# TensorE's slot re-ordered in a two-layer attention kernel: transposed probabilities first, out-projections behind them, the next scores ahead of the weighting of values

## What is computed

```python
h = tok(x, W)                                             # (64, 49, 768) @ (768, 192)
h = layernorm(h + attn1(h))                               # layer 1
h = layernorm(h + attn2(h))                               # layer 2
# attn1: softmax(q k^T + q rel^T, causal) v, then w_proj
# attn2: probs = softmax(h @ Wg.T + bg); combine = its best two, scattered
#        delta = einsum((h @ A + ba) * combine, Bm) + combine @ bb, times 2
#        qkv = h @ Wqkv.T + bqkv + delta; softmax(q k^T / 4) v, then Wproj
```

## Time and profile before

| what | value |
|---|---|
| runs | 397.36, 398.04, 395.19 us |
| the profiled execution | 395.62 us, of which span 393.8 us, mean granted TensorE clock 0.999 of full speed |
| TensorE matmul busy | 374.1 us, 95% of the span |
| TensorE weight load busy | 327.7 us, 83% |
| VectorE, ScalarE, GpSimd busy | 303.0, 217.8, 126.0 us |
| chain of waits, by engine | TensorE 82%, VectorE 5%, ScalarE 4%, issue 3%, DMA 2%, GpSimd 2% |
| DMA rate in the first two slices of 9.85 us | 265 and 230 GB/s |

### The profile page before, as it was taken

One profiled execution on the slowest core, in us unless ns is written; L12 is line 12 of the kernel. 1 busy time (PEld: TensorE's weight loads), 2 busy tenths in 40 slices (PEclk: granted clock), 3 DMA queues, 4 the chain that ended last, 5 costly groups with the idle time before them and its releaser, 6 DMA issues.

```text
span 393.8 us, 13738 instructions
## 1 busy us (share of the span) xinstructions
PE 374.1 (95%) x5312; PEld 327.7 (83%) x5312; DVE 303.0 (77%) x814; ACT 217.8 (55%) x692; POOL 126.0 (32%) x262
## 2 busy tenths in 40 slices
PE   5989999999999999999999999999999999898984
PEld 5778878988889888988898889888888988777874
DVE  7366678677777878987878888697788888697872
ACT  1245565655646646565655566655664665564542
POOL 1222431431323514232324333342324342323332
PEclk9999999999999999999999999999999999999999
DMA  8623421222132112320022201111011101111111
GB/s 265 230 59 102 136 54 20 71 54 50 17 75 55 25 28 69 100 59 9 17 67 68 67 8 29 19 29 21 21 18 30 27 21 19 19 32 17 27 30 37
DMA packets 49338, 20.68 MB, mean 53 GB/s; under 512 B 41262, under 2 KB 45713, under 8 KB 49274
## 3 DMA queue, kind: packets, MB, share of 16 engines
q1 hardware_dynamic: 45386, 10.04, 12.3%
q10 hardware_dynamic: 3888, 9.77, 7.7%
HBM read 12.57 MB, written 2.41 MB: 38 GB/s over the span
## 4 chain that ended last, share of the span: by engine, by line
PE 82%; DVE 5%; ACT 4%; issue 3%; DMA 2%; POOL 2%; SPq 1%; POOLq 0%; ACTq 0%; DVEq 0%
PE ps L474 11%; PE ps L547 9%; PE ps L574 9%; PE ps L585 7%; PE ps L559 6%; PE ps L596 5%; PE ps L524 4%; PE ps L528 4%; PE ps L526 4%; PE ps L597 4%; DMA add<-in_add 2%; PE ps L504 2%; PE ps L510 2%; PE ps L541 2%; PE ps L617 2%
## 5 line engine op out<-in xcount | busy, mean ns | idle before, releaser
L927 DVE TENSOR_REDUCE psum<-probs 113x12 f32<-113x588 f32 x64 | 48.7, 760 | 35.0 <-ACT probs L778 35.0
L792 ACT COPY pt<-ps 113x339 f32<-113x339 f32 x128 | 50.2, 445 | 34.7 <-PE ps L574 34.1
L901 DVE TENSOR_REDUCE mx<-ps 113x12 f32<-113x588 f32 x64 | 48.7, 761 | 18.4 <-PE ps L547 17.7
L429 POOL TENSOR_SCALAR shift<-mv,rstd 128x1 f32<-128x1 f32 (+1 forms) x50 | 14.0, 280 | 149.7 <-ACT rstd L827 149.7
L474 PE MATMUL ps<-tokw,xs 128*128 128x192 f32 (+1 forms) x300 | 56.3, 336 | 4.1 <-DMA tokw<-in_tokw 3.9
L418 POOL TENSOR_SCALAR kbd<-k,const 64x294 f32<-64x294 f32 x64 | 35.0, 557 | 65.1 <-ACT q L771 62.8
L474 PEld LDWEIGHTS ps<-tokw,xs 128*128 128x128 f32 (+1 forms) x300 | 48.9, 192 | 7.0 <-DMA xs<-in_x 4.3
L574 PE MATMUL ps<-const,probs 113*113 113x113 f32 x384 | 49.8, 266 | 3.0 <-DVE probs L936 2.5
L936 DVE TENSOR_TENSOR probs<-probs,rsum 113x588 f32<-113x588 f32 x64 | 49.8, 778 | 2.2
L908 DVE TENSOR_TENSOR probs<-ps,mx 113x588 f32<-113x588 f32 x64 | 49.4, 772 | 2.2
L574 PEld LDWEIGHTS ps<-const,probs 113*113 113x113 f32 x384 | 44.4, 178 | 7.4 <-issue 6.7
(11 more groups left out here) (93 smaller groups left out, 789.0 us busy)
## 6 DMA issues: line engine op xcount, KB each, us to landing
xs<-in_x ACTq DMA_DIRECT2D x23, 384.0 KB, 4.8
vbd<-vrow SPq DMA_DIRECT2D x160, 18.4 KB
out<-o SPq DMA_DIRECT2D x24, 96.0 KB, 1.7
tokw<-in_tokw ACTq DMA_DIRECT2D x3, 192.0 KB, 3.5
w<-in_w SPq DMA_DIRECT2D x1, 472.5 KB, 4.3
xs<-in_x SPq DMA_DIRECT2D x3, 128.0 KB, 3.3
xs<-in_x SPq DMA_DIRECT2D x1, 384.0 KB, 5.8
add<-in_add SPq DMA_DIRECT2D x1, 361.5 KB, 9.4
```

Source lines behind the costliest of these rows:

```text
L792: nc.scalar.copy(pt[n % 2][:, 3 * half:3 * half + 3, :].rearrange("p g i -> p (g i)"), ps[0:PP, 2 + half, 0:3 * PP]).then_inc(pt_ready[hal ...
L901: nc.vector.tensor_reduce(mx[:].rearrange("p (b h) -> p b h", b=2), score_view, AX.X, ALU.max).then_inc(mx_ready, 1)
L927: nc.vector.tensor_reduce(psum[:].rearrange("p (b h) -> p b h", b=2), probs_view(n), AX.X, ALU.add).then_inc(sum_ready, 1)
```

## The change

1. **TensorE's slot.** It now begins with `transpose_h` and `transpose_probs(n-1)`; `out1` and `out2` follow. The scores of chain n+1 stand ahead of `weigh_values` of chain n-1 (except in `fresh` slots, and chain 63, whose scores are computed in slot 62 right behind the transposes, into banks 4 and 5).
2. **GpSimd.** `block_diagonal(n+2)` goes ahead of `normalise` where its k was projected in an earlier slot.
3. **Start.** x of block 2 is issued by SP ahead of `add1`; x of blocks 3 and 4 by ScalarE only behind the first `take_h`. The embedding of slot 1 is also split around `transpose_h`.
4. **End.** Largest value, subtraction and exponential of chain 63 are done in slot 62 (VectorE before the sum of chain 62; `mx` has two buffers). The out-projection of block 21 moves from slot 62 to 63. Blocks 22 and 24 (`urgent`) project q and k ahead of v, and copy q ahead of v. `keep_busy` uses bank 7.

```diff
@@ planner
-    spread(QKV2, 19, lambda b: (ROUTED[b] + 1, max(ROUTED[b] + 1, SLOT2[first_use(b)] - 2 + (SLOT2[first_use(b)] > len(CHAINS) - 6))))
+    spread(QKV2, 19, lambda b: (ROUTED[b] + 1, max(ROUTED[b] + 1, SLOT2[first_use(b)] - 2 + (len(CHAINS) - 6 < SLOT2[first_use(b)] < len(CHAINS) - 1))))
-OUT2 = [n + 2 + (n + 2 in [m + 2 for m in DONE1]) for n in DONE2]
+OUT2 = [n + 2 + (n + 2 in [m + 2 for m in DONE1] + [len(CHAINS) - 2]) for n in DONE2]
+def urgent(b):
+    return SLOT2[first_use(b)] - QKV2[b] <= 1 or b == BLOCKS - 1
+def score_bank(n):
+    return 4 if n == LAST else 0
@@ sync
             sp.dma_start(w1b[:], w1b_in).then_inc(w1b_loaded, 16)
+            sp.dma_start(xs[:, 2], x[2]).then_inc(x_loaded[2], 16)
             sp.dma_start(add1[:], add1_in).then_inc(add1_loaded, 16)
@@ gpsimd
+                layer, t = attention(n + 2)
+                known = bool(layer and (QKV1 if layer == 1 else QKV2)[block_of(t)] < n)
+                if known:
+                    block_diagonal(n + 2)
                 for b in out1(n):
                     normalise(L1, b, h[0:tokens(b), b, :])
...
-                block_diagonal(n + 2)
+                if not known:
+                    block_diagonal(n + 2)
@@ tensor
             for n in range(FIRST, SLOTS):
                 before, u = attention(n - 1)
-                for b in out1(n):
...
-                    bank6 = out_project(L1, p1, b, SLOT1, bank6)
...
-                split = bool(n <= 0 and turns(n))
+                split = bool(n <= 1 and turns(n))
...
                     transpose_probs(n - 1, bank3)
                     if n >= LAST:
                         keep_busy(3)
+                    if n == LAST - 1:
+                        scores(L2, attention(LAST)[1], LAST)
+                for b in out1(n):
...
+                    bank6 = out_project(L1, p1, b, SLOT1, bank6)
...
+                        bank6 = out_project(L2, p2, b, SLOT2, bank6)
                 for b in turns1(n):
...
+                    if urgent(b):
+                        bank4 = project_qk2(b, bank4)
                     bank5 = project_v(L2, b, values2(b), bank5)
-                    bank4 = project_qk2(b, bank4)
+                    if not urgent(b):
+                        bank4 = project_qk2(b, bank4)
...
+                layer, t = attention(n + 1)
+                fresh = bool(layer == 2 and block_of(t) in qkv2s(n))
+                if layer and not fresh and n + 1 < LAST:
+                    scores(L1 if layer == 1 else L2, t, n + 1)
                 if before == 1:
                     weigh_values(L1, u, n - 1)
...
-                if layer and not fresh:
-                    scores(L1 if layer == 1 else L2, t, n + 1)
@@ scalar
-            for b in range(2, XS):
-                load_x(b)
...
+                if b == 0:
+                    for late in range(3, XS):
+                        load_x(late)
...
                 if before:
                     take_y(n - 1, u)
+                if n == LAST - 1:
+                    exponent(LAST)
@@ vector
+                if n == LAST - 1:
+                    largest(LAST)
+                    subtract(LAST)
```

More of the change, by code:

```diff
@@ L275, in build @@
         pt = [sb(f"pt{u}", [PP, 6, PP]) for u in range(2)]
-        mx = sb("mx", [PP, H])
+        mx = [sb(f"mx{u}", [PP, H]) for u in range(2)]
         psum = sb("psum", [PP, H])
@@ L534, in scores @@
                 if n > 0:
[L535 removed]
+                    if n == LAST:
+                        pe.wait_ge(L2.qk_ready, BLOCKS)
+                        pe.wait_ge(L2.v_rows, BLOCKS)
+                    else:
+                        pe.wait_ge(sub_ready, n)
                 else:
@@ L634, in keep_busy @@
             def keep_busy(count):
-                pe.wait_ge(L2.qk_ready, BLOCKS)
+                pe.wait_ge(hw_ready, BLOCKS)
                 for _ in range(count):
-                    nc.tensor.matmul(ps[:, 4, 0:128], ident, ident, start=True, stop=True)
-            LAST = len(CHAINS) - 1
+                    nc.tensor.matmul(ps[:, 7, 0:128], ident, ident, start=True, stop=True)
             bank3 = bank4 = bank5 = bank6 = None
@@ L677, in _ @@
                         keep_busy(3)
+                    if n == LAST - 1:
+                        scores(L2, attention(LAST)[1], LAST)
+                for b in out1(n):
+                    if b == 0:
+                        pe.wait_ge(p1_loaded, 16)
+                        pe.wait_ge(ones_ready, 1)
+                    bank6 = out_project(L1, p1, b, SLOT1, bank6)
+                bare = bool(routers(n) and not turns(n) and not qkv2s(n) and not embeds(n))
+                if not bare:
+                    for b in out2(n):
+                        if b == 0:
+                            pe.wait_ge(p2_loaded, 16)
+                        if n > LAST:
+                            keep_busy(2)
+                        bank6 = out_project(L2, p2, b, SLOT2, bank6)
                 for b in turns1(n):
@@ L836, in _ @@
                     take_ht(b)
-                if n <= 0 and turns(n):
+                if n <= 1 and turns(n):
                     for b in embeds(n):
@@ L845, in _ @@
                     act.wait_ge(masks_ready, 1)
-                if layer:
+                if layer and n < LAST:
                     exponent(n)
@@ L850, in _ @@
                 for b in qkv2s(n):
-                    take_v(L2, b, 0, SLOT2)
+                    if not urgent(b):
+                        take_v(L2, b, 0, SLOT2)
                     take_k2(b)
-                    if turns(n) or embeds(n):
+                    if turns(n) or embeds(n) or urgent(b):
                         take_q2(b)
+                    if urgent(b):
+                        take_v(L2, b, 0, SLOT2)
                 for b in turns(n):
                     take_v(L1, b, NB, SLOT1)
-                if not (n <= 0 and turns(n)):
+                if not (n <= 1 and turns(n)):
                     for b in embeds(n):
@@ L861, in _ @@
                     take_y(n - 1, u)
+                if n == LAST - 1:
+                    exponent(LAST)
                 if not turns(n) and not embeds(n):
                     for b in qkv2s(n):
-                        take_q2(b)
+                        if not urgent(b):
+                            take_q2(b)
                 for b in out1(n):
@@ L989, in _ @@
                     router_max(b)
-                if layer:
+                if layer and n < LAST:
                     largest(n)
                     subtract(n)
+                if n == LAST - 1:
+                    largest(LAST)
+                    subtract(LAST)
                 for b in out1(n):
                     add_residual(L1, b)
-                for b in out2(n):
-                    add_residual(L2, b)
+                if n != LAST:
+                    for b in out2(n):
+                        add_residual(L2, b)
                 for b in out1(n):
```

26 lines of the change are left out of this document (8 added, 18 removed).

## The result

| | before | after |
|---|---|---|
| median of 5 runs each | 397.35 us (395.19 to 398.04) | 436.68 us (431.49 to 441.38) |
| profiled execution, its span | 395.6, 393.8 us | 441.38, 439.6 us |
| mean granted clock | 0.999 | 0.958 |

The changed kernel is slower, by a ratio of 1.093 (95% interval 1.087 to 1.099). Two of its five runs, 441.38 (the profiled one) and 439.71 us, fell into a slower state; ratios, and the medians of the table of experiments, leave such runs out (there also single outliers up to 1996 us), and without them the median here is 432.55 us.

The account below looks back on a forecast made before the run. TensorE's issued work plus its few waits was taken as the bound. Terms +14.8 +17.2 -2.4 -2.4 -1.4 = +25.8 us on the profiled 395.6 gave 421.4, named as 421; range 405 to 430 (8 in 10).

Parts of the forecast that it names:

- Odd boundaries, +14.8: Odd slot boundaries: transposes wait barely covered for ScalarE's copy of y out of bank 2; +14.8 us.
- Even boundaries, +17.2: Ends of even slots: transposes wait for bank 3, emptied by take_hw behind take_y and take_q2; +17.2 us.
- The scores ahead, 0 in themselves: Scores ahead of the weighting: same instructions, so no cost in themselves; 0 us, bounds -2 and +2.
- Transposes ahead of out-projections: VectorE's residual comes some 0.7 us later in the slot but stays hidden, as exponential and sum end later.
- second cover, 0.75 us: Out-projection ahead of the transposes, taken to cover ScalarE's take_y for 0.75 us; moving it removes that cover.
- GpSimd and blocks 22 and 24, -2.4: Waits of scores for the block-diagonal k vanish, -3.0 us; late softmax in short slots, +0.6; net -2.4.
- start, -2.4: Kernel start: earlier add1, -1.5 us; half an embedding filling slot 1's wait, -0.9; together -2.4.
- end, -1.4: Last two chains: transposes 2.4 instead of 4.92 us apart, less 1.1 for chain 62; -1.4 us.
- The bound of 2.7 us: Start: most that delaying 0.77 MB of x, at 265 GB/s, could win for add1; up to 2.7 us.
- Only bank 2 costs: Rival: take_hw done in time, so even boundaries lose only 1.6 and some 1 us; 407 us, chance 0.14.
- Faster: Rival: softmax starts 0.5 us earlier, removing TensorE's waits, and the copy yt is hidden; 386 us, chance 0.06.
- It cancels: Rival: waits are a third of the sums, +10 against -6.2 at the ends; 399 us, chance 0.04.

Follow-up runs that it names:

- h: Changed kernel with the bank of the weighted values alternating between 2 and 3, so half of the next transposes goes to a free bank: 420.93 us.
- k: Changed kernel with the alternating bank and ScalarE's take_hw ahead of take_q2 and inverse_deviation: 419.85 us.
- n: Changed kernel with the alternating bank, take_hw ahead of take_q2 on ScalarE, and the transposes of h1 later in the slot: 401.20 us.
- o: Changed kernel with only the transposes of h1 (and take_h1) later in the slot, in another bank in some slots: 419.93 us.
- a: Changed kernel with the scores put back behind the weighting of values, all else of the change kept: 408.04 us.
- b: Kernel before with only the scores moved ahead of the weighting of values: 429.04 us.
- g: Changed kernel with both TensorE orders put back (out-projections first, scores behind the weighting), all else of the change kept: 392.90 us.
- f: Changed kernel with three idle matmuls ahead of the transposes of probabilities in slots 54 to 62: 429.68 us.
- g2: Kernel g with the start's edit undone too: 394.51 us.
- j: Kernel g with the alternating bank for the weighted values: 391.07 us.
- p: Kernel j with the transposes of h1 later in the slot: 386.95 us.
- l: Kernel k with three idle matmuls ahead of the transposes in slots 54 to 62: 422.93 us.

## Why the prediction was right and wrong

- **The step that failed: the end.** The sum has it at about -1.0 us, at the full clock; it took +15.3. What the runs showed in its place stands under "The term that was missing".
- **Odd boundaries, +14.8.** Right in the mechanism and its times (0.98 against 1.07, 2.53 against 2.55). The step also said that `transpose_h1` at 2.55 sets the time wherever there is an out-projection. My expectation for h forgot that, and so did k's; n and o confirm it.
- **Even boundaries, +17.2.** Right: 1.97 against 1.94 at the place measured. The steps forecast for slots 1 to 54 come to 13.6 (odd, without boundaries 55 and 61) + 12.8 (even, without 54 and later) - 0.9 (half an embedding at the first q/k/v) = 25.5. Measured: 24.2.
- **The scores ahead, 0 in themselves.** Too low. Busy time in slots 1 to 54 grew by 2.0 us (301.7 against 299.7), the upper bound that the step gave; from a to the changed kernel, where the scores alone move, it grew by 3.1 (from 298.6). But the prediction took scores and out-projection for two covers of the same copy. By b the scores alone cost nearly all (23.3 us in slots 1 to 54), since the out-projection waits for y too.
- **Transposes ahead of out-projections, "It stays hidden".** The residual was not hidden: TensorE waits 2.9 us for h in a, 1.1 in g. And the "second cover, 0.75 us" was none for `take_y` but one for probabilities and hw: 7.0 us between g and a in slots 1 to 54. The sum of the middle was right all the same, since with both orders changed the waits lie on top of each other. That was luck: nothing in the prediction provided for it.
- **GpSimd and blocks 22 and 24, -2.4; start, -2.4; end, -1.4.** Right in sign, too large in sum: g shows -4.5 for all of them. The end is 1.0 us shorter in g. The last two chains' transposes came to stand 4.12 us apart in g and 3.56 in f, not 2.4. The start's edit is worth 1.6: against g2, slot 1's transposes come 0.6 later and slots 1 to 54 are 2.1 shorter, so nothing was won by an earlier `add1`, and all of it by the work put into the wait (slot 2's transposes follow slot 1's by 3.98 us in g, by 6.01 in g2). The bound of 2.7 us was also mis-sized: 0.77 MB at 265 GB/s is 2.9 us. In the changed kernel slot 1 came 2.8 us later; the clock rose at 13.4 instead of 7.1, and f, with the same start and the rise at 7.4, has slot 1 at 24.3.
- **The term that was missing.** The sum prices every step at the full clock. The end was forecast at about -1.0 (waits of 0.5, 1.2 and 0.1, less 1.4, less 1.4 for the block-diagonal k) and measured +15.3. Of the 16.3 between them, f shows 11.3 to be the half clock. The other 5.0 are in f too, whose end is 46.65 at nearly full clock. 2.0 of them lie behind the last transposes, where the out-projections now stand ahead of the last weighting (11.7 us against 9.6), a place for which the sum has no term; the other 3 are waits in slots 58 to 62 put too low, with the idle matmuls of f among them. With the start's 2.5 that is 14 us of clock in the profiled execution, which accounts for most of the 20.0 by which it missed the sum (45.8 against 25.8). Of the 11.6 us by which the median of 432.55 missed the forecast, the clock near the end is 3 to 6, by f, and the waits at the end, no longer than in f, up to 5. No row of before showed a clock below full in the middle, but the sum itself had put the longest waits (1.24 and 1.74 us at boundaries 54, 57 and 60) into the shortest slots. That was the place to set a rival.
- **The pages.** The alternating bank is the rotation that the Trainium skill, Perfetto Trace Analysis, section Optimizing Tensor Performance, asks for. It won 11.6 us where the copy was bare (h; 7.2 of them in slots 1 to 54) and 1.8, within the spread of the runs, where it was covered (j). By the rule of the Trainium skill, Trainium Kernel Development and Optimization, section Performance Expectations, as the prediction read it, much could still be filled at a weight-load share of 83%. All the edits of p together found 11 us against before, and the share only came to 85%; the waits were the better guide to how much was there.
- **The rivals.** *Only bank 2 costs* fell: the even waits are there. *Faster* fell: the transposes wait 0.43 us for y and start 0.98 after the weighting. *It cancels* fell.

## What to carry to other kernels

Before two pieces of work change places, ask for each whether it can really run while the latency in question passes: an out-projection that reads y is no cover for the copy of y, but it is one for the probabilities. When waits lie on top of each other, removing one uncovers the next, so single repairs under-report (7.2, 4.1 and 7.9 us for a total of 23.9), and one can be worth more than the waits listed for it (the later transposes of h1: 7.9 us, where 4.4 were listed). And a sum that puts its longest waits into short slots needs a rival in which TensorE's clock falls, worked out at half speed for the stretch behind them.

## What the runs showed of the hardware that I had not expected

- The granted clock fell to 1.2 GHz in the middle of busy work, behind waits of 1.1 to 1.5 us, for 13.7 and 20.5 us. It cost 11.3 us in the profiled execution, and 3 to 6 in the runs of the table. By the Trainium skill, TensorE: Matmul & The Clock Gate, section "HAM oscillation — how this bites in real kernels", waits for DMA between short groups of matmuls let the clock fall again and again. The trace agrees that it falls repeatedly (0.50 in two stretches near the end, 1.00 between them); but the waits here were for copies and probabilities, and none was longer than 1.5 us. 27 idle matmuls, placed in those waits, took it away; placed elsewhere they did not; in a kernel with fewer waits (l) they did not take all of it away.
- How often it falls differs between runs of one kernel: the five runs of the changed kernel had mean clocks of 0.958 to 0.983 and times of 441.4 to 431.5 us, in that order. The kernels with few waits (g, j, p) had 0.996 or more in every run and spread over 1.2 to 3.3 us.
- At the start the clock rises at about 7 to 10 or at about 13 us, with either version of the start, and the later rise costs 2 to 3 us (slot 1 at 24.3 in f and at 27.3 in the changed kernel, with the same start).
